# A vision-tower kernel on one core: set-up loads reordered, weight products put into the first step, and the order inside a step changed

## The chip, the cores and the metric

The kernel runs on one core of one Trainium2 chip. Its engines are TensorE (PE: matrix products and transposes; PEld is its load of weights), VectorE (DVE), ScalarE (ACT), GpSimd (POOL) and SyncE (SP, which issues transfers). Each works through its own list of instructions in order and waits for the others by semaphores. The metric is the time of one execution in microseconds of device time.

## The reference

64 images of 2 x 104 x 104 are shifted four ways by 4 pixels and stacked to 10 channels, normalised over the whole stack, multiplied by `gamma`, added to `beta` and convolved in 8 x 8 patches to 169 tokens of 128. Then an attention layer with exponential features and a feed-forward layer in which each token goes to 2 of 8 experts, both behind a layer norm and added to their input:

```
normed = (concat - mean) * rsqrt(var + EPS) * gamma + beta      # statistics over the 10 shifted channels
h = conv(normed, W, stride 8) + b                               # (64, 169, 128)
xn = layernorm(h);  q, k, v = heads(xn @ Wqkv.T)                # 8 heads of 64
qf = exp((q * scale) @ proj.T);  kf = exp(k @ proj.T)
out = (qf @ (kf.T @ v)) / (qf @ sum(kf) + 1e-6)
h = h + out @ Wout.T + bout
y = layernorm(h); top-2 of y @ Wg; softmax of the two           # expert: silu(y @ W[e]) * (y @ V[e]) @ W2[e]
h = h + sum over the two experts of weight * expert(y)
```

## The kernel before, in words

The program has three stages. The **set-up** loads the first group of 8 images, the constants and the weights; computes the image statistics of group 0 (`image_stats`, `image_var`, `image_shift`; GpSimd does the root); turns `gamma`, `beta` and the convolution weights with transposes (`turn_maps`; results `gam`, `bT`, `wct`); folds `proj` into the query and key weights (`qk_mm`, L470, split into a high and a low part `wqp`, `wkp`), and the value weights into the output weights (`vo_mm`, L480, result `wvo`); and makes the patches of group 0 in seven **front pieces**: TensorE transposes normalised rows (L433), VectorE multiplies them by `gam` into `patches` (L761). `cbeta`, the convolution of beta, comes from five products at L492.

The **steps** n = 0 to 34 are a software pipeline over 32 pairs of images. In one step four pairs are in work: pair n (`a`: convolution L555, first layer norm, tokens `xtok`, L878), pair n-1 (`b`: query features in four products `q_feature(0..3)` and key features in three `k_tokens(0..2)`, L643 to L645, each followed by an exponential on ScalarE, then the context), pair n-2 (`c`: the denominators `d8`, L548; VectorE makes their reciprocals `rparts`; `broadcast(0..3)`, L506, spreads them over partitions; `normalise(0..3)`, L812, multiplies; the output products L605; second layer norm) and pair n-3 (`d`: choice of experts, and rows scattered to DRAM by GpSimd). Steps go in groups of four (k = 0 to 3). Beside them runs the front of the next group: statistics in k = 0, and its pieces in k = 1, 2, 3 at the four places `front(0..3)` of a step. The order of every engine is written out by hand in its own `step` function. TensorE uses banks 4 and 5 in turn for the features, banks 7 and 1 for the broadcasts.

The **experts** stage (from about 700 us) is a loop over 92 tiles of sorted rows. It isn't touched.

Transfers of the set-up are issued by SP, by ACT (half of the images) and by POOL (`gamma`, `beta`). The second group of images is issued by SP at its step 0, once `norm_done` has come to 3 (first group normalised). ScalarE sums up that group with `image_sums` (L1014 to L1024) and `image_squares` (L1030, L1032).

## Time and profile before

| | us |
|---|---|
| median of 3 runs (1181.48 to 1183.8) | 1181.81 |
| the profiled execution, its own time | 1181.96 |
| its span, first to last instruction | 1180.2 |
| first convolution (end of set-up) | from 41.35 |
| convolution of step 1, of step 2 | from 57.59, 74.91 |
| PE busy | 1086.5 (92%) |
| DVE, ACT, POOL busy | 877.7, 559.5, 630.3 |

All times are microseconds from the span's start. In a timeline a row is a run of like instructions: start, length, engine, line, operation, out<-in, form, count, and in brackets how long the engine had been idle before it and whose instruction ended that. Matrix products are pipelined, so successive rows of PE overlap: the time that one takes from TensorE is the distance to the next start.

### The profile page before, as it was taken

How to read it: one execution, taken by the hardware profiler on the slowest of the kernel's cores; microseconds unless marked ns; L12 is line 12 of the kernel's file. 1: busy time of each engine (PE TensorE's matmuls, PEld its weight loads, DVE VectorE, ACT ScalarE, POOL GpSimd, SP SyncE). 2: the span in 40 equal slices, each digit the busy share in tenths (PEclk: the TensorE clock that was granted, in tenths of full speed). 3: DMA queues.
4: the chain of work that ended last, by engine and by line, in shares of the span. 5: the costliest groups of instructions: out<-in, count | busy, mean ns of one | idle time of the engine just before them, and what ended most of it. 6: DMA issues, size and time to landing. Idle time of an engine off the chain costs nothing.

```text
span 1180.2 us, 30003 instructions
## 1 busy us (share of the span) xinstructions
PE 1086.5 (92%) x8568; PEld 918.4 (78%) x8569; DVE 877.7 (74%) x3313; ACT 559.5 (47%) x1303; POOL 630.3 (53%) x666
## 2 busy tenths in 40 slices
PE   2699999999999999999999728999999999999994
PEld 2567777777677777777777528999999999999994
DVE  4448788787787878878867666777777777777773
ACT  3243634535436354354333314555555555555551
POOL 2001535354535354545354653777777777677774
PEclk9799999999999999999999958999999999999998
DMA  9252130120301312201010432443444444444442
...
DMA packets 75793, 65.56 MB, mean 56 GB/s; under 512 B 12382, under 2 KB 66718, under 8 KB 75712
## 3 DMA queue, kind: packets, MB, share of 16 engines
...
q14 instruction: 40, 0.33, 0.1%
...
## 4 chain that ended last, share of the span: by engine, by line
PE 68%; issue 13%; DVE 8%; POOL 3%; DMA 1%; ACT 1%; POOLq 0%; DVEq 0%; ACTq 0%; SPq 0%
PE bank L1278 22%; PE bank L1290 13%; PE bank L605 7%; PE bank L669 4%; PE bank L656 3%; PE bank L662 3%; PE bank L555 3%; PE bank L643 2%; DVE patches L761 2%; DVE xtok L878 2%; PE bank L433 2%; DVE attn L812 2%; PE bank L1266 2%; POOL rstd L1150 2%; PE bank L644 2%
## 5 line engine op out<-in xcount | busy, mean ns | idle before, releaser
L1405 POOL DMA_INDIRECT out_rows<-yo,dest x184 | 329.0, 1788 | 139.7 <-issue 94.1
L1278 PE MATMUL bank<-xT_e,wv 128*128 128x256 f32 x2208 | 289.3, 287 | 0.9 <-DVE xT_e L1355 0.9
L1278 PEld LDWEIGHTS bank<-xT_e,wv 128*128 128x128 f32 x2208 | 272.4, 190 | 1.3 <-DVE xT_e L1355 1.3
L1175 POOL DMA_INDIRECT sorted_rows<-xrow_all,sloti x192 | 187.6, 977 | 62.2 <-issue 54.9
L1329 ACT ACTIVATE sil<-bank 128x256 f32<-128x256 f32 x368 | 141.7, 385 | 160.4 <-PE bank L1278 160.4
L1290 PE MATMUL bank<-w,hid 128*128 x1472 | 179.5, 275 | 1.0 <-DVE hid L1362 1.0
L1148 POOL TENSOR_SCALAR vare<-mv 128x3 f32<-128x3 f32 x64 | 12.5, 195 | 303.3 <-issue 249.4
L1290 PEld LDWEIGHTS bank<-w,hid 128*128 128x128 f32 x1472 | 171.6, 192 | 1.2 <-issue 1.2
L1362 DVE TENSOR_TENSOR hid<-sil,bank 128x256 f32<-128x256 f32 x368 | 145.3, 417 | 29.0 <-ACT sil L1329 25.0
L1344 DVE TENSOR_TENSOR wv<-wv_all,wv 128x1024 fp32r<-128x1024 f32 x92 | 112.8, 1226 | 64.6 <-PE bank L1278 62.8
L1313 ACT CAST wv<-wv_all 128x1024 fp32r x92 | 96.2, 1046 | 38.0 <-issue 30.1
L1088 ACT ACTIVATE attn<-bank 128x256 f32<-128x256 f32 x128 | 49.4, 386 | 131.1 <-PE bank L645 131.1
L555 PE MATMUL bank<-patches,wct 128*128 128x338 f32 x320 | 101.9, 466 | 2.3 <-DVE patches L761 2.3
L761 DVE TENSOR_TENSOR patches<-bank,gam 128x416 f32<-128x416 f32 (+3 forms) x160 | 71.7, 503 | 26.4 <-PE bank L433 25.5
L605 PE MATMUL bank<-attn 128*128 128x169 f32 x512 | 83.6, 317 | 7.1 <-DVE attn L812 7.1
L605 PEld LDWEIGHTS bank<-attn 128*128 128x128 f32 x512 | 76.0, 193 | 13.4 <-DVE attn L812 13.2
L555 PEld LDWEIGHTS bank<-patches,wct 128*128 128x128 f32 x320 | 59.7, 194 | 31.5 <-issue 4.3
L1103 ACT ACTIVATE attn<-bank 128x512 f32<-128x512 f32 x96 | 57.3, 598 | 51.5 <-PE bank L645 50.3
L669 PE MATMUL bank<-wvo,attn 128*64 128x136 f32 x1024 | 75.9, 287 | 1.9 <-ACT attn L1123 1.0
L1083 ACT COPY attn<-bank 128x272 f32<-128x272 f32 x128 | 50.0, 390 | 42.6 <-PE bank L669 39.6
L1123 ACT COPY attn<-bank 128x512 f32<-128x512 f32 x32 | 18.7, 586 | 103.9 <-PE bank L662 103.9
L656 PE MATMUL bank<-attn,xtok 128*128 128x512 f32 x128 | 67.9, 612 | 0.0
...
## 6 DMA issues: line engine op xcount, KB each, us to landing
...
```

Of the source, the lines that this page charges most:

```text
L555: t = pe.matmul(bank[1][:, 0:PT], wct[:, q], patches[:, par, q, 2 * k:2 * k + 2].rearrange("p b t -> p (b t)"), start=(q == 0), stop=(q == 4))
L605: t = pe.matmul(bank[7][:, TOK * i:TOK * i + TOK], mm[:, pc, i, j, 0:D], qf[:, pc, j, TOK * i:TOK * i + TOK], start=(j == 0), stop=(j == 3))
L656: pe.matmul(bank[(6, 1)[i]][:, :], xtok[:, p, i], kf[:, i], start=True, stop=False)
L669: t = pe.matmul(o_[64 * (h % 2):64 * (h % 2) + 64, col:col + D + HEADS], gT[:, i, NF * h:NF * h + NF], wvo[:, h], start=True, stop=True)
L1175: po.indirect_dma_start(sorted_rows, bass.IndirectOffsetOnAxis(sloti[:, p, j, ch:ch + 1], 0), xrow[:, p, j, ch], None).then_inc(s(f"scatte ...
L1278: q = pe.matmul(bank[fc][:, TT * m:TT * m + TT], wv[:, w, w_, m, cols], xT[:, p, x_], start=(w_ + x_ == 0), stop=(w_ == 1))
L1290: q = pe.matmul(bank[4 + p][:, D * a:D * a + D], hid[:, p, fc, 128 * a:128 * a + 128], w2[:, bass.ds(e, 1), fc].rearrange("p e n -> p (e n ...
L1313: ac.copy(wv[:, w, 0].rearrange("p m n -> p (m n)"), wv_all[:, bass.ds(e, 1)].rearrange("p e m n -> p (e m n)")).then_inc(s("w_high"), 1)
L1329: ac.activation(sil[:, fc % 2], bank[fc][:, 0:TT], ACT.Silu).then_inc(s("silu_done"), 1)
L1344: ve.tensor_tensor(wv[:, w, 1].rearrange("p m n -> p (m n)"), wv_all[:, bass.ds(e, 1)].rearrange("p e m n -> p (e m n)"), wv[:, w, 0].rear ...
L1362: ve.tensor_tensor(hid[:, p, fc], sil[:, fc % 2], bank[fc][:, TT:2 * TT], ALU.mult).then_inc(s("h_done"), 1)
L1405: po.indirect_dma_start(out, bass.IndirectOffsetOnAxis(dest[:, p, a:a + 1], 0), yo[:, p, a], None, compute_op=ALU.add).then_inc(s(f"added{ ...
```

## The change

On SP the set-up loads come in another order: images, then only the first 358 columns of the constants (the segment `mhalf` is moved up; the rest comes later under a semaphore of its own, `kept_in`), `gamma`, `proj`, the rows, the convolution weights, `beta`, and only then the attention weights. `gamma` and `beta` leave POOL's queue for SP's. VectorE does the image statistics ahead of gamma. TensorE no longer makes the folded weights between the front pieces: `query_key_weights` and `output_weights` run inside step 0, and what VectorE and ScalarE do for them too (`late_weights`, and `image_sums` of group 1 behind `output_weights`). In every step, TensorE's order of query products, broadcasts and key products is another, VectorE's `normalise` calls are spread out, and of `normal_rows` only the small `scaled_gaps` stays early: the rest comes behind `front(2)`.

```diff
-            sp.dma_start(cst[:], const[:, 0:NKEPT]).then_inc(s("const_in"), 16)
-            sp.dma_start(wc_raw, convw.rearrange("e (g c) y x -> e g (c y x)", g=5)).then_inc(s("wc_in"), 16)
+            sp.dma_start(cst[:, 0:NEARLY], const[:, 0:NEARLY]).then_inc(s("const_in"), 16)
+            load_map(sp, graw, gamma, s("gamma_in"))
             for t in range(2):
...
+            load_rows(sp, 0)
+            sp.dma_start(wc_raw, convw.rearrange("e (g c) y x -> e g (c y x)", g=5)).then_inc(s("wc_in"), 16)
+            load_map(sp, braw, beta, s("beta_in"))
+            sp.dma_start(convb_sb[:], convb.rearrange("(d a) -> d a", a=1)).then_inc(s("convb_in"), 16)
+            sp.dma_start(qkv_raw, wqkv.rearrange("(t j e) d -> e t j d", t=3, e=128)).then_inc(s("qkv_in"), 16)
             sp.dma_start(wo_raw, wout.rearrange("o (j e) -> o j e", j=4)).then_inc(s("wo_in"), 16)
-            load_rows(sp, 0)
-            sp.dma_start(qkv_raw, wqkv.rearrange("(t j e) d -> e t j d", t=3, e=128)).then_inc(s("qkv_in"), 16)
-            sp.dma_start(wg_sb[:], wg).then_inc(s("wg_in"), 16)
-            sp.dma_start(convb_sb[:], convb.rearrange("(d a) -> d a", a=1)).then_inc(s("bias_in"), 16)
-            sp.dma_start(bout_sb[:], bout.rearrange("(d a) -> d a", a=1)).then_inc(s("bias_in"), 16)
+            sp.dma_start(cst[:, NEARLY:], const[:, NEARLY:NKEPT]).then_inc(s("kept_in"), 16)
             sp.dma_start(selr, const[:, NKEPT:]).then_inc(s("sel_in"), 16)
             sp.dma_start(tokid[:], const[:, SEG["tok"][0]:SEG["tok"][1]]).then_inc(s("tok_in"), 16)
+            sp.dma_start(wg_sb[:], wg).then_inc(s("wg_in"), 16)
+            sp.dma_start(bout_sb[:], bout.rearrange("(d a) -> d a", a=1)).then_inc(s("bout_in"), 16)
...
-            sp.wait_ge(s("const_in"), 16)
-            sp.dma_start(sorted_rows[E * CAP:E * CAP + TT].rearrange("(a p) n -> p a n", a=2), pad).then_inc(s("pads_out"), 16)
...
+                if n == 1:
+                    sp.wait_ge(s("kept_in"), 16)
...
             pe.wait_ge(s("const_in"), 16)
+            image_stats(0)
+            pe.wait_ge(s("pj_in"), 32)
...
             pe.wait_ge(s("gamma_patched"), 1)
             for half in range(2):
                 turn_maps(bank[5 + half], 0, half).then_inc(s("gamma_mm"), 1)
-            image_stats(0)
...
+            front(0)
             pe.wait_ge(s("wc_in"), 16)
...
-            front(0)
             front(1)
-            pe.wait_ge(s("qkv_in"), 16)
-            pe.wait_ge(s("pj_copied"), 2)
+            front(2)
             pe.wait_ge(s("gam_copied"), 2)
-            for t in range(2):
-                for j in range(4):
...
-            front(2)
             pe.wait_ge(s("beta_patched"), 1)
             turn_maps(bank[6], 1, 0).then_inc(s("beta_mm"), 1)
-            pe.wait_ge(s("wo_copied"), 2)
...
-            for jj in range(2):
...
-            pe.wait_ge(s("wg_in"), 16)
...
             front(4)
-            front(5)
+            pe.wait_ge(s("wc_copied"), 2)
             pe.wait_ge(s("beta_copied"), 2)
             for g in range(5):
...
+            front(5)
             front(6)
-            pe.wait_ge(s("vo_copied"), 2)
...
+            def query_key_weights():
+                pe.wait_ge(s("qkv_in"), 16)
...
+                        mm_ = pe.matmul(bank[4 + t][:, 128 * j:128 * j + 128], qkv_raw[:, t, j], pjT, start=True, stop=True)
+                    mm_.then_inc(s("qk_mm"), 1)
+                pe.wait_ge(s("wo_in"), 16)
...
+                    mm_ = pe.transpose(bank[6][:, 128 * j:128 * j + 128], wo_raw[:, j], ident)
+                mm_.then_inc(s("wo_mm"), 1)
...
+            def output_weights():
+                pe.wait_ge(s("wo_copied"), 2)
...
+                        mm_ = pe.matmul(bank[6 + jj][:, 256 * (j % 2):256 * (j % 2) + 256], wv_c[:, j],
...
+                pe.matmul(bank[2][:, 384:384 + E], ones, wg_sb[:], start=True, stop=True).then_inc(s("gate_mean"), 1)
...
                 if b:
-                    for j in range(2, 4):
-                        pe.wait_ge(s("q_exp"), 4 * mb + j - 1)
-                        q_feature(j)
+                    pe.wait_ge(s("q_exp"), 4 * mb + 1)
+                    q_feature(2)
+                if d and not a and not b:
+                    rank()
+                if c:
+                    pe.wait_ge(s("rden_ready"), mc + 1)
+                    broadcast(0)
                 if a:
...
+                if n == 0:
+                    query_key_weights()
+                if b:
+                    pe.wait_ge(s("q_exp"), 4 * mb + 2)
+                    q_feature(3)
                 front(0)
-                if d and not a and not b:
-                    rank()
                 if c:
-                    pe.wait_ge(s("rden_ready"), mc + 1)
-                    broadcast(0)
-                    if a:
-                        pe.wait_ge(s("h1_ready"), n + 1)
                     broadcast(1)
...
+                for j in range(NCH):
+                    if b:
+                        if j < 2:
+                            pe.wait_ge(s("q_exp"), 4 * mb + 3 + j)
+                        else:
+                            pe.wait_ge(s("k_exp"), NCH * mb + 1)
                         k_tokens(j)
-                for j in range(2, 4):
-                    if c:
-                        pe.wait_ge(s("qn_done"), 4 * mc + j - 1)
-                        broadcast(j)
-                    if b and j < NCH:
-                        pe.wait_ge(s("k_exp"), NCH * mb + j - 1)
-                        k_tokens(j)
+                    if c and j < 2:
+                        pe.wait_ge(s("qn_done"), 4 * mc + j + 1)
+                        broadcast(j + 2)
...
+                if n == 0:
+                    output_weights()
...
+            image_var(0)
+            ve.wait_ge(s("gamma_in"), 16 * 5)
...
+            image_shift(0)
...
-            image_var(0)
-            ve.wait_ge(s("wc_mm"), 1)
-            ve.tensor_copy(wct[:, 0:4].rearrange("p g k -> p (g k)"), bank[1][:, :]).then_inc(s("wc_copied"), 1)
-            image_shift(0)
...
-                    ve.wait_ge(s("qkv_in"), 16)
-                    for j in range(4):
...
-            for t, scale in ((0, QS), (1, 1.0)):
-                ve.wait_ge(s("qk_high"), t + 1)
...
+                    ve.wait_ge(s("wc_mm"), 1)
+                    ve.tensor_copy(wct[:, 0:4].rearrange("p g k -> p (g k)"), bank[1][:, :]).then_inc(s("wc_copied"), 1)
...
+            def output_weights():
+                ve.wait_ge(s("qkv_in"), 16)
+                for j in range(4):
+                    t = ve.tensor_scalar(wv_c[:, j], qkv_raw[:, 2, j], qkv_raw[:, 2, j, D - 1:D], None, ALU.subtract)
...
+                ve.wait_ge(s("wo_mm"), 1)
+                for h in range(2):
+                    ve.tensor_copy(woT[64 * h:64 * h + 64, :, h], bank[6][64 * h:64 * h + 64, :].rearrange("p (j n) -> p j n", j=4)
...
+            def late_weights():
+                for t, scale in ((0, QS), (1, 1.0)):
+                    ve.wait_ge(s("qk_high"), t + 1)
...
+                    ve.scalar_tensor_tensor(out=lo, in0=bank[4 + t][:, :], scalar=scale, in1=hi.bitcast(F32),
...
+                ve.tensor_copy(ident_gate[:, 0:D], ident)
+                ve.wait_ge(s("kept_in"), 16)
...
+                ve.tensor_copy(pick_head[:], selr[0:104].rearrange("p (j f) -> p j f", j=4)).then_inc(s("pick_copied"), 1)
+                ve.wait_ge(s("gate_mean"), 1)
+                ve.scalar_tensor_tensor(out=ident_gate[:, D:], in0=bank[2][:, 384:384 + E], scalar=-1.0 / D, in1=wg_sb[:],
...
+                def scaled_gaps():
+                    ve.wait_ge(s("ln2_rstd"), md + 1)
+                    ve.tensor_tensor(gaps[:], gap[:], rstd[:, 1], ALU.mult).then_inc(s("gap_ready"), 1)
...
-                if d and a:
-                    normal_rows()
...
+                if d and a:
+                    scaled_gaps()
...
+                if c:
+                    normalise(0)
                 if a:
                     ve.wait_ge(s("h1t_done"), n + 1)
                     norm_stats(lambda ch: bank[2][:, D * ch:D * ch + D], 0, n, s("ln1_bn"), s("ln1_mv"))
+                if n == 0:
+                    output_weights()
                 if c:
-                    normalise(0)
                     normalise(1)
                 front(0)
+                if c:
+                    normalise(2)
...
                 if c:
-                    normalise(2)
                     normalise(3)
...
+                if n == 0:
+                    late_weights()
...
+                if d and a:
+                    normal_rows()
...
-                ac.wait_ge(s("qk_mm"), half + 1)
-                ac.mul((wqp, wkp)[half][:, 0], bank[4 + half][:, :], (QS, 1.0)[half]).then_inc(s("qk_high"), 1)
...
+            def query_key_weights():
+                for t in range(2):
+                    ac.wait_ge(s("qk_mm"), t + 1)
+                    ac.mul((wqp, wkp)[t][:, 0], bank[4 + t][:, :], (QS, 1.0)[t]).then_inc(s("qk_high"), 1)
...
+            def output_weights():
+                for jj in range(2):
+                    ac.wait_ge(s("vo_mm"), jj + 1)
+                    ac.copy(wvo[:, 4 * jj:4 * jj + 4, 0:D], bank[6 + jj][:, :].rearrange("p (h n) -> p h n", h=4)
...
-                if fr and k == 0:
+                if n == 0:
+                    query_key_weights()
+                if fr and k == 0 and n > 0:
                     image_sums(g + 1)
...
+                if n == 0:
+                    output_weights()
+                    image_sums(g + 1)
...
-            for raw, src, done in ((graw, gamma, s("gamma_in")), (braw, beta, s("beta_in"))):
-                for q in range(5):
-                    po.dma_start(raw[NP1 * q:NP1 * (q + 1)], src[C * q:C * q + C].rearrange("c (y k) x -> y c k x", k=PATCH)
```

TensorE, step 2, behind the third query product of pair 1 (bank 4); before, the fourth query product, the transposes of `h1T`, both broadcasts and then keys:

```order
L643 MATMUL bank5<-xT,wqp 128x362
L644 MATMUL bank5<-xT,wqp 128x362
L645 MATMUL bank5<-xT,wqp 128x362
L568 MATMUL bank2<-cst,h1T 128x128 x3
L506 MATMUL bank7<-rparts,pick_head 128x340
L506 MATMUL bank1<-rparts,pick_head 128x340
L643 MATMUL bank4<-wkp,xT 128x512
L644 MATMUL bank4<-wkp,xT 128x512
L645 MATMUL bank4<-wkp,xT 128x512
L643 MATMUL bank5<-wkp,xT 128x512
L644 MATMUL bank5<-wkp,xT 128x512
L645 MATMUL bank5<-wkp,xT 128x512
```

and now (the three lines of a product, L643 to L645, are L664 to L666 here, the broadcast is L522):

```order
L522 MATMUL bank7<-rparts,pick_head 128x340
L589 MATMUL bank2<-cst,h1T 128x128 x3
L664 MATMUL bank5<-xT,wqp 128x362
L665 MATMUL bank5<-xT,wqp 128x362
L666 MATMUL bank5<-xT,wqp 128x362
L522 MATMUL bank1<-rparts,pick_head 128x340
L664 MATMUL bank4<-wkp,xT 128x512
L665 MATMUL bank4<-wkp,xT 128x512
L666 MATMUL bank4<-wkp,xT 128x512
L522 MATMUL bank7<-rparts,pick_head 128x340
L664 MATMUL bank5<-wkp,xT 128x512
L665 MATMUL bank5<-wkp,xT 128x512
```

The first broadcast moved ahead of the `h1T` transposes, the fourth query product behind them, and each later broadcast stands behind one key product instead of two.

ScalarE, end of the set-up and step 0, before (`wqp`, `wkp`, `wvo` are the folded weights, `edges`/`edge_out`/`colsum` the statistics of group 1):

```order
L1066 COPY patches<-bank6 128x7x5x13
L1070 ACTIVATE wqp<-bank4 128x512
L1066 COPY patches<-bank6 128x6x5x13
L1070 ACTIVATE wkp<-bank5 128x512
L1073 COPY wvo<-bank3 128x4x128
L1073 COPY wvo<-bank1 128x4x128
L1014 ACTIVATE edges<-raw44 112x16x4 x2
L1021 ACTIVATE nrm44,colsum<-raw44 112x1664
L1024 ACTIVATE edge_out,colsum<-edges 112x128
L1115 CAST xT<-bank3 128x384
L1030 ACTIVATE nrm44,colsum<-raw44 112x1664
L1032 ACTIVATE edge_out,colsum<-edges 112x128
```

and now:

```order
L1105 COPY patches<-bank6 128x6x5x13
L1112 ACTIVATE wqp<-bank4 128x512
L1112 ACTIVATE wkp<-bank5 128x512
L1161 CAST xT<-bank3 128x384
L1117 COPY wvo<-bank6 128x4x128
L1117 COPY wvo<-bank7 128x4x128
L1053 ACTIVATE edges<-raw44 112x16x4 x2
L1060 ACTIVATE nrm44,colsum<-raw44 112x1664
L1063 ACTIVATE edge_out,colsum<-edges 112x128
L1069 ACTIVATE nrm44,colsum<-raw44 112x1664
L1071 ACTIVATE edge_out,colsum<-edges 112x128
```

The folded weights moved to either side of the `xT` copy of step 0, and the sums of group 1 behind them.

VectorE, step 0 from its first convolution, before:

```order
L862 TENSOR_TENSOR h1T<-bank1,cbeta 128x256
L862 TENSOR_TENSOR h1T<-bank1,cbeta 128x2x41
L767 BN_STATS bns<-bank2 128x6 x3
L770 BN_AGGR mv<-bns 128x2 x3
L878 TENSOR_SCALAR xtok<-bank2,mv,rstd 128x128 x3
L890 MEMSET xtok 128x3
L892 TENSOR_TENSOR xT<-bank3,xT 128x384
L703 TENSOR_SCALAR part<-colsum,cst 112x2
L706 SCALAR_TENSOR_TENSOR part<-colsum,cst,part 112x2
```

and now:

```order
L891 TENSOR_TENSOR h1T<-bank1,cbeta 128x256
L891 TENSOR_TENSOR h1T<-bank1,cbeta 128x2x41
L781 BN_STATS bns<-bank2 128x6 x3
L784 BN_AGGR mv<-bns 128x2 x3
L801 TENSOR_SCALAR patches<-xrow_all 128x128 x4
L805 COPY patches<-bank6 64x4x128 x2
L914 TENSOR_SCALAR xtok<-bank2,mv,rstd 128x128 x3
L925 MEMSET xtok 128x3
L927 TENSOR_TENSOR xT<-bank3,xT 128x384
L812 SCALAR_TENSOR_TENSOR wqp<-bank4,wqp 128x512
L812 SCALAR_TENSOR_TENSOR wkp<-bank5,wkp 128x512
```

The value weights (L801) and the turned output weights (L805, which wait for TensorE) now stand ahead of `xtok`, and the low halves of `wqp` and `wkp` behind `xT`.

## Rows read from the trace of the kernel before

**Rows 1.** The page, part 4: the chain that ended last, shares of the span.
```profile
PE 68%; issue 13%; DVE 8%; POOL 3%; DMA 1%; ACT 1%; POOLq 0%; DVEq 0%; ACTq 0%; SPq 0%
```

**Rows 2.** Window of step 5; busy us (instructions) of each engine, TensorE clock, DMA.
```profile
210.50:230.16 19.66, 19.04 (x149) 14.02 (x145) 16.45 (x76) 10.73 (x23) 9.41 (x15) 1.00 0.10 31
```

**Rows 3.** Timeline of step 5: start, length, engine, line, operation.
```profile
210.50 3.11 PE L555 MATMUL bank<-patches,wct 128*128 128x338 f32 x10
...
213.70 0.58 DVE L862 TENSOR_TENSOR h1T<-bank,cbeta 128x256 f32<-128x256 f32 x2
...
213.95 0.33 PE L643 MATMUL bank<-xT,wqp 128*128 128x362 f32 x1
...
214.44 0.49 PE L568 MATMUL bank<-cst,h1T 128*128 128x128 f32 x3
...
214.69 0.56 PE L506 MATMUL bank<-rparts,pick_head 104*128 104x340 f32 x2
...
215.09 0.40 PE L643 MATMUL bank<-wkp,xT 128*128 128x512 f32 x1
...
216.04 1.24 ACT L1103 ACTIVATE attn<-bank 128x512 f32<-128x512 f32 x2 [0.89 <-PE bank L645]
...
218.36 0.92 DVE L812 TENSOR_TENSOR attn<-attn,bank 128x338 f32<-128x338 f32 x2
...
218.52 0.53 PE L649 MATMUL bank<-cst,xtok 128*128 128x128 f32 x3
...
219.33 2.56 PE L605 MATMUL bank<-attn 128*128 128x169 f32 x16 [0.28 <-DVE attn L812]
```

**Rows 4.** Timeline of step 7, TensorE alone.
```profile
258.31 0.49 PE L649 MATMUL bank<-cst,xtok 128*128 128x128 f32 x3
258.64 0.52 PE L433 MATMUL bank<-cst,nrm 104*128 104x104 f32 x4
```

**Rows 5.** Waits in steps 4 to 30: us in total, times, longest.
```profile
PEld bank L605 <- DVE attn L812: 10.4, 20, 0.5
```

**Rows 6.** Timeline of step 32, TensorE alone.
```profile
663.87 0.42 PE L506 MATMUL bank<-rparts,pick_head 104*128 104x340 f32 x1 [0.43 <-DVE attn L812]
```

**Rows 7.** Timeline of the set-up.
```profile
18.25 1.89 DVE L696 TENSOR_REDUCE colsum<-raw 112x1 f32<-112x1664 f32 x1 [2.58 <-DMA raw<-in_x]
...
24.25 3.72 ACT L1042 ACTIVATE nrm<-raw,imgshift,imgrstd 112x832 f32<-112x832 f32 x3 [3.59 <-DVE imgshift L719]
...
25.16 1.41 DVE L744 COPY patches<-bank 64x512 f32<-64x512 f32 x2
...
28.77 3.50 PE L470 MATMUL bank<-patches,xrow_all 128*128 128x128 f32 x16
...
32.92 1.94 PE L480 MATMUL bank<-patches 128*128 128x256 f32 x8
...
39.51 1.57 ACT L1021 ACTIVATE nrm<-raw 112x1664 f32<-112x1664 f32 x1
...
41.35 4.77 PE L555 MATMUL bank<-patches,wct 128*128 128x338 f32 x10 [2.27 <-DVE patches L761]
```

**Rows 8.** Windows of the set-up, columns as in rows 2.
```profile
0.00:10.00 10.00, 0.00 (x0) 0.01 (x1) 4.42 (x13) 1.30 (x2) 6.90 (x16) 1.00 0.72 127
10.00:18.00 8.00, 0.00 (x0) 0.00 (x1) 1.02 (x1) 0.00 (x0) 0.00 (x0) 1.00 1.05 161
```

**Rows 9.** Timeline of step 0 and the start of step 1.
```profile
46.85 0.55 PE L568 MATMUL bank<-cst,h1T 128*128 128x128 f32 x3 [0.74 <-DVE h1T L862]
...
49.91 1.05 DVE L878 TENSOR_SCALAR xtok<-bank,mv,rstd 128x128 f32<-128x128 f32 x3 [1.36 <-POOL rstd L1150]
...
52.33 1.59 ACT L1030 ACTIVATE nrm<-raw 112x1664 f32<-112x1664 f32 x1
...
54.87 0.54 PE L419 MATMUL bank<-part,cst 112*112 112x2 f32 x2 [2.96 <-DVE part L706]
```

**Rows 10.** Window in step 0, columns as in rows 2.
```profile
51.00:56.00 5.00, 2.03 (x8) 1.63 (x9) 1.23 (x5) 2.35 (x5) 0.00 (x0) 0.50 0.00 0
```

104 lines of the change are left out of this document (47 added, 57 removed).

## The prediction

> **What bounds the kernel now.** The chain that ended last comes first: TensorE holds 68% of it, issue 13%, VectorE 8% [rows 1], so a gain has to shorten TensorE's list or a stretch in which TensorE waits. The window of one step shows which: in step 5 TensorE is busy for 19.04 of 19.66 us at the full clock of 2.4 GHz, VectorE for 16.45 [rows 2]. The experts' loop isn't touched. Two places are left: small waits inside a step, of which there are some thirty, and the 57 us up to the convolution of step 1. The reader is to look in the timelines for the distance between starts on TensorE, which shows a stall even where the idle time in brackets is small.
>
> **Inside a step.** The second layer norm's `xtok` stands between VectorE's second and third `normalise`, so the last one ends late: two of them run 218.36 to 219.28, and the output products begin at 219.33, although the three transposes before them began at 218.52 [rows 3]. In step 7, where a front piece stands between, the same three take 0.33 [rows 4]. So TensorE stalls 219.33 - 218.52 - 0.33 = 0.48; I take 0.45, since the switch of kind costs a little too. The list of waits has this one 20 times, 10.4 us in all on the weight loads [rows 5]: every step with k = 0, 1, 2. With steps 2, 31 and 28 to 30 outside or inside that window, 23 steps have it.
>
> The new order does `normalise(2)` while VectorE would wait for GpSimd's root, so only `normalise(3)` (half of 0.92) stands behind `xtok`. Laid out for step 5 from rows 3: third query product until 213.95 (there the fourth began), first broadcast until 214.15 (two took 215.09 - 214.69 = 0.40). `h1T` is written 213.70 to 214.28, so the transposes now wait until about 214.33, a new stall of 0.2 that the fourth query product covered before. Then transposes 0.25 to 0.33, fourth query product 0.5, broadcast, and from there the same work as before. The fourth product moved behind costs 214.44 - 213.95 = 0.5, the broadcast moved ahead gives back 0.2, the transposes begin 0.1 earlier, a further change between kinds of product costs 0.1: TensorE reaches the output products's place 0.3 later in pure work, or 0.25 without the small stall in front of the third broadcast that goes. The stall of 0.45 goes fully, as `normalise(3)` then ends near 218.8 and TensorE comes at 218.95. And two products no longer queue up for one `normalise`, another 0.1. Net gain 0.45 + 0.1 - 0.25 = 0.3 (bounds 0.1 and 0.45) in 23 steps: **-7.0**.
>
> In k = 3 with a front piece (7 steps) there is no stall to win [rows 4] and the price stays: 0.25 each, **+1.8** (0 to 3).
>
> `normal_rows` (0.85, three products on VectorE) leaves the head of the step, where it stood ahead of `dsum`, for the place behind `front(2)`. VectorE has 3.2 us free in the step [rows 2], and the row work now lies where it waits for ScalarE's copy of h2; its end is late by at most 0.85, and the same 0.85 no longer stands ahead of the reciprocals. GpSimd copies the rows later and comes to its root of the second norm up to 0.7 later; `scaled_gaps`, which waits for that root, has moved behind the `h1T` addition, over 3 us on. I cost it at 0; if the cover were gone it would be 0.7 in each of the steps, the upper end of a bad case below. The wait for the scatters in `place` is met a step earlier.
>
> In step 32 there is no convolution to hide things: the second key product now stands behind the third broadcast, which waits for VectorE until 663.87 [rows 6]; that product takes 0.7 (0.49 for the 362 columns of a query product [rows 3], here 512). **+0.7**. Steps together: -7.0 + 1.8 + 0.7 = **-4.5**.
>
> **The set-up.** Statistics need the images and a piece of the constants. They landed by 18.25 [rows 7]. By 18 us 10 x 127 + 8 x 161 KB = 2.56 MB had moved [rows 8]. Now eight images (80 KB each), the edges (53 KB) and 358 columns of constants (183 KB) stand at the heads of two queues: 0.86 MB, which at 161 GB/s from 2 us on are in at 7.3. Transfers don't fill all engines alike, and I take 10 (bounds 7.5 and 13): images 8.25 earlier.
>
> On this the skill has two sentences. The Trainium skill, DMA: Bandwidth & Descriptors, "Issuing engines are not separate DMA queues", says that transfers of all issuing engines interleave on the same 16; the trace's share of 1.05 with three queues open agrees, so two queues lose nothing. The section on why a DMA increments its semaphore by 16 says that a copy from SP or ACT runs on the largest number of engines up to 16 that divides its outer size: 12 for an image, 13 for a map. No run here shows that; as an estimate by that page the images would come at 2 + 0.86 / (0.161 x 12/16) = 9.1 instead of 7.3, inside my bounds, and the maps, moved to SP, would gain nothing from the move.
>
> From landing to the first normalisation are 24.25 - 18.25 = 6.0, unchanged: 16.0. From there to the first convolution were 17.1 [rows 7]. The query/key products (3.50) and value/output products (1.94) leave this stretch, which would make it 11.7. But `beta` now lies behind 0.86 MB, `gamma` (0.43), `proj` (0.03), the rows (0.68) and the convolution weights (0.33), with its own 0.43 some 2.8 MB deep, which is 19 us at the same rate and by the uneven filling more likely 23; its copy, maps, the five products of `cbeta` and two front pieces with VectorE's multiplications behind them follow. That makes about 34.5, and bounds of 28 and 37. Conv starts **-6.9**.
>
> Step 0 gives it back. Before, from the start of the `h1T` transposes to that of the statistics of group 1, which stand ahead of step 1 on TensorE, were 54.87 - 46.85 = 8.0 [rows 9]. Two additions:
> 1. `xtok` waits for 0.55 of transposes, the query/key products, four transposes and VectorE's 1.41 [rows 7]. At full clock (1.75 + 0.5) it starts 4.2 after 46.85, at half (3.50 + 1.1) 6.6; before 3.06. So +1.15 or +3.5.
> 2. Between `xtok` and ScalarE's squares were 52.33 - 49.91 = 2.4. Now: `xtok` 1.05, transposes 0.5, output products 1.94 (or twice), copy 0.54, sums of group 1 about 2.3 (1.57 of it in rows 7, where ScalarE did them in idle time): 6.3 or 8.7. So +3.9 or +6.3.
>
> Together +5.1 at 2.4 GHz, +9.8 at 1.2. Low-halves and other late weights on VectorE lie beside the sums. The convolution itself, 4.77 here [rows 7] against 3.11 in step 5 [rows 3], may gain 1.3 at full clock. Sum for the set-up: -6.9 - 1.3 + 5.1 = -3.1, or -6.9 + 9.8 = +2.9. The clock decides: in step 0 it is granted at 0.50 with TensorE busy for 2.03 of 5.00 us [rows 10]. TensorE: Matmul & The Clock Gate (the Trainium skill, "What's actually happening") says that the clock is set by how busy the array has recently been; the row agrees, and by that rule the products at the front of step 0 run warm behind the convolution and the output products, behind an idle wait, cold. That is in between, and I take **-1** (bounds -5 and +5).
>
> **Sum.** -4.5 - 1 = -5.5 on the profiled execution's 1181.96 (span 1180.2 and 1.8 around it), which is 0.15 above the median: **1176.4**.
>
> **The rivals.**
> - *The set-up pays.* If images land at 8 and the clock stays up, it gives -6 rather than -1, and the steps 0.35 each: 1170. For it: SP's order of need. Against: the serial stretch of step 0, over 5 us at either clock.
> - *The steps give nothing*: `h1T` is the wait that takes the place, 0.45 in all of 30 steps instead of 0.2, and with it the late k products. Then steps +1, set-up -1: 1182. For it: VectorE wrote `h1T` right behind the reciprocals, so any delay goes through. Against: the list of steps' waits has it small.
> - *Slower: ScalarE's exponentials.* The second key product needs the exponential of the fourth query product, now begun 1 us later, and the third key product that of the first key, in two banks. From rows 3: query product ends 215.4, its exponential (0.5, by its columns and the 0.62 of a key's) 215.95, while TensorE comes at 216.2; margin 0.25. The two key exponentials took 1.24, so the next margin is 0.2. If the exponentials come 0.5 later than I lay out, both margins are gone and each step loses 0.6 instead of gaining 0.3: 30 x 0.3 + 7 x 0.6 more, with the set-up +2: 1191. It decides from 0.3 us on.
>
> **Chances.** My forecast 50%, set-up pays 22%, no gain 16%, exponentials 12%. A difference below 0.2% (2.4 us) can't be told from none here. The forecast (1172 to 1180) lies nearly all below 1179.4; with the first rival that makes faster 0.70, same 0.17, slower 0.13. The range takes in the bounds of the set-up and half of the slower case: 1168 to 1184.
>
> **What would show it.** Output products start 0.33 behind the `xtok` transposes in k = 0 to 2, with a gap of 0.2 before the `h1T` transposes; group distance 0.7 us shorter over four steps. Image landing near 10, first convolution near 34.5, step 1's statistics product near 54. It is wrong if the gap between third query product and transposes is over 0.4, if TensorE waits for ScalarE before a key product, or if step 1's convolution starts over 3 us from 57.

## The result and the profile after

The changed kernel took 1170.55 us (median of 4 runs, 1169.45 to 1171.41), the kernel before 1182.12 beside it (1181.48 to 1183.8): ratio 0.9897, 95% interval 0.9882 to 0.9913, 11.6 us less where 5.5 had been forecast. The profiled execution took 1170.11 us, with a span of 1168.3. In the chain that ended last TensorE went from 68% to 84% [rows 1]. This share is no measure of the gain: it moved by 16 points and the span by 1%.

```profile
PE 84%; DVE 6%; issue 3%; DMA 2%; ACT 2%; SPq 1%; POOL 1%; POOLq 0%; ACTq 0%; DVEq 0%
```

The gain inside a step shows in step 5, to be read against [rows 3]. Those rows and [rows 2] are headed step 5, but the convolution that they begin with, at 210.50, is that of step 9 ([rows 4] is step 11, not 7). The comparison holds all the same: step 5 of the kernel before, from 132.75 on, also took 19.66, and reached the transposes of `xtok` after 8.03. First the window after (distance, then busy us of TensorE, its weight loads, VectorE, ScalarE, GpSimd; clock, DMA share, GB/s), 19.29 where 19.66 was [rows 2]:

```profile
130.12:149.41 19.29, 18.93 (x149) 14.01 (x145) 15.99 (x74) 10.76 (x23) 9.63 (x16) 1.00 0.10 32
```

Then its timeline on TensorE (start, length, line, operation). L522 is the broadcast, L589 the transposes of `h1T`, L670 those of `xtok`, L626 the output products:

```profile
133.56 0.31 PE L522 MATMUL bank<-rparts,pick_head 104*128 104x340 f32 x1
133.90 0.55 PE L589 MATMUL bank<-cst,h1T 128*128 128x128 f32 x3
134.20 0.42 PE L664 MATMUL bank<-xT,wqp 128*128 128x362 f32 x1
...
138.23 0.49 PE L670 MATMUL bank<-cst,xtok 128*128 128x128 f32 x3
138.58 1.70 PE L626 MATMUL bank<-attn 128*128 128x169 f32 x10
```

The output products start 0.35 behind the transposes of `xtok`, not 0.81. The transposes of `h1T` begin 0.34 behind the first broadcast, which takes 0.16 (134.78 to 134.94 for the next): the new wait is 0.18, and 0.2 was forecast. Up to the transposes of `xtok` TensorE needs 8.11 from the start of the step and needed 8.02 [rows 3]: the new order costs it 0.09, not 0.25. The waits of the whole span say the same (us in total, times, longest), first before, then after:

```profile
PEld bank L605 <- DVE attn L812: 13.2, 25, 1.0
PEld bank L506 <- DVE attn L812: 9.9, 25, 1.2
...
PEld bank L568 <- DVE h1T L862: 3.5, 11, 1.4
```

```profile
PEld bank L589 <- DVE h1T L891: 11.0, 32, 1.3
...
PEld bank L522 <- DVE attn L840: 2.5, 2, 1.6
...
PEld bank L626 <- DVE attn L840: 1.0, 1, 1.0
```

Two waits for `normalise` nearly go, that of the output products (13.2 to 1.0) and that of the third broadcast (9.9 to 2.5); the one for `h1T` (3.5 to 11.0) takes their place, shorter and in every step.

The set-up after, to be read against [rows 7] and [rows 9]:

```profile
11.12 1.89 DVE L714 TENSOR_REDUCE colsum<-raw 112x1 f32<-112x1664 f32 x1 [5.44 <-DMA raw<-in_x]
...
22.81 1.58 ACT L1101 COPY wv_all<-attn 65x1664 f32<-65x1664 f32 x1 [1.32 <-DMA attn<-in_L_tok_beta]
...
33.68 4.76 PE L572 MATMUL bank<-patches,wct 128*128 128x338 f32 x10 [2.29 <-DVE patches L775]
...
44.92 1.89 PE L506 MATMUL bank<-patches 128*128 128x256 f32 x8
...
47.64 1.58 ACT L1060 ACTIVATE nrm<-raw 112x1664 f32<-112x1664 f32 x1
...
49.69 1.59 ACT L1069 ACTIVATE nrm<-raw 112x1664 f32<-112x1664 f32 x1
...
52.31 0.54 PE L430 MATMUL bank<-part,cst 112*112 112x2 f32 x2 [5.37 <-DVE part L724]
...
55.03 4.25 PE L572 MATMUL bank<-patches,wct 128*128 128x338 f32 x10
```

The images are there at 11.12 (was 18.25), the first convolution starts at 33.68 (41.35), step 1's at 55.03 (57.59). Step 0 gives back 5.1 of 7.7, and the row for L430 shows where most of it goes: TensorE idles for 5.37 behind the output weights while ScalarE sums and squares group 1.

Three marks divide every run here: the convolution of step 2, the last convolution (step 31's), the end of the span.

```
start of conv, us      step 2    step 31   between     behind
before                 74.91     637.74    562.83      542.5
after                  73.09     626.08    552.99      542.2
```

So 1.8 of the 11.9 in the span lie ahead of step 2, 9.8 in steps 2 to 30, 0.2 behind. These are marks of one profiled execution each. How far they move by themselves, kernels with the same code in a stretch show: between the marks 562.8 and 563.2 with the old steps (before, and s2 below), 552.8 to 553.4 with the new ones (changed kernel, s1 and i2 below). A single step can be 0.3 off.

### The profile page after: what moved, and what is told of

Its sections match the earlier page's. It is cut to its first block, busy times and chain, and to the rows that moved or that the text cites. A ratio compares the mean times of both kernels' runs of the same rounds, so it can differ in the third digit from the quotient of the medians.

```text
span 1168.3 us, 29989 instructions
## 1 busy us (share of the span) xinstructions
PE 1082.7 (93%) x8568; PEld 920.1 (79%) x8569; DVE 879.2 (75%) x3313; ACT 560.7 (48%) x1303; POOL 624.7 (53%) x656
## 4 chain that ended last, share of the span: by engine, by line
PE 84%; DVE 6%; issue 3%; DMA 2%; ACT 2%; SPq 1%; POOL 1%; POOLq 0%; ACTq 0%; DVEq 0%
PE bank L1324 22%; PE bank L1336 13%; PE bank L572 8%; PE bank L626 5%; PE bank L690 4%; PE bank L664 4%; PE bank L677 4%; PE bank L666 4%; PE bank L665 4%; DVE patches L775 3%; PE bank L683 2%; PE bank L444 2%; PE bank L565 2%; PE bank L522 2%; PE bank L1312 2%
## 5 line engine op out<-in xcount | busy, mean ns | idle before, releaser
L626 PE MATMUL bank<-attn 128*128 128x169 f32 x512 | 81.2, 311 | 0.6 <-DVE attn L840 0.6
L690 PE MATMUL bank<-wvo,attn 128*64 128x136 f32 x1024 | 75.9, 287 | 2.3 <-ACT attn L1172 1.4
L626 PEld LDWEIGHTS bank<-attn 128*128 128x128 f32 x512 | 75.5, 192 | 2.0 <-DVE attn L840 1.0
L1147 ACT ACTIVATE attn<-bank 128x512 f32<-128x512 f32 x96 | 57.3, 598 | 33.8 <-PE bank L666 33.8
L690 PEld LDWEIGHTS bank<-wvo,attn 128*64 128x64 f32 x1024 | 56.7, 136 | 14.6 <-ACT attn L1127 6.9
```

The source lines that it names most:

```text
L626: t = pe.matmul(bank[7][:, TOK * i:TOK * i + TOK], mm[:, pc, i, j, 0:D], qf[:, pc, j, TOK * i:TOK * i + TOK], start=(j == 0), stop=(j == 3))
L690: t = pe.matmul(o_[64 * (h % 2):64 * (h % 2) + 64, col:col + D + HEADS], gT[:, i, NF * h:NF * h + NF], wvo[:, h], start=True, stop=True)
```

## Experiments

Ratios are to the kernel before on the same chip, with 95% intervals. On two chips every kernel was slower, that before too (1254 and 1281 us), and the traces of the changed ones there show VectorE and ScalarE starting late from step 4 on. Ten of the eighteen runs fell there, and of them only times up to the end of step 3 are used. s1 is all step edits on the old set-up, s2 the new set-up alone, s3 and s5 one step edit each, i2 the changed kernel with one more move:

```
kernel (runs)     step 2   step 3   ratios on these two chips
s1 (1)            19.02    19.36    0.9979
s2 (2)            19.51    19.32    0.9987, 0.9930
s3 (3)            19.11    19.30    0.9963, 0.9975, 0.9979
s5 (2)            19.50    19.54    1.0212, 1.0276
i2 (2)            step 2 begun at 71.86, 70.56; ratios 0.9799, 0.9815
before, elsewhere 19.52    19.30
```

These early steps already tell s3 (0.4 gained in step 2) from s5 (nothing there, 0.24 lost in step 3). What had been expected, in the order of the runs, is quoted here; whatever it says of the end of the kernel these runs leave open.

The first four were to settle where the gain lies. Beyond step 3 they settle nothing: the "9 us faster" of s1 and s3 did not show on that chip, and s5's loss did:

> The kernel before with all the changes to the order inside a step (TensorE's, the early third normalisation, the late row work) and its old set-up. Theory T: the steps' gain stands by itself and is 9.8 us from step 2 on, so this run is 9 to 10.5 us faster than the kernel before (about 1172), with the output products 0.33 behind the transposes of xtok in k = 0 to 2. Rival A (my forecast's sizes hold and the rest of the gain comes from the set-up, whose early arrivals help the steps too): 4 to 5.5 us faster (about 1177). Rival B (most comes from the two parts together): under 3 us.

> The changed kernel with the steps in the order of before: the set-up's change alone. Theory T: step 1's convolution starts 2.6 us earlier and its own step is 0.7 longer at the low clock, so 1.5 to 2.5 us faster than the kernel before (about 1180). Rival A: 6 us or more faster (about 1175). Rival B: between -1 and +1 us, its gain given back within the first steps.

> The kernel before with one thing moved: VectorE does the third normalisation ahead of xtok instead of behind it. TensorE's order stays. Theory T (the stall of 0.48 behind the transposes of xtok and a slow restart of 0.1 are what the steps gained, and the new order on TensorE costs and gives nothing): 23 steps x 0.4 to 0.55 = 9 to 12 us faster. Rival P (TensorE's new order is needed, since in the old one the third normalisation is asked of VectorE while it has the reciprocals' and xtok's inputs to serve, and xtok comes later for it): xtok is 0.45 late and its transposes wait as long, so within 2 us of the kernel before.

> The kernel before with TensorE's new order alone; VectorE's and the set-up stay. Theory T (price of the order per step is 0.0 to 0.1, as read in the changed kernel; the stall of 0.48 stays, for VectorE's third normalisation still stands behind xtok): between 1 us faster and 3 us slower. Rival Q (the order itself gives: two broadcasts no longer queue up): 3 to 6 us faster. Rival R (my forecast's price of 0.25 in 30 steps holds and was hidden by VectorE's change): 6 to 8 us slower.

Run again, with the same late starts, with steps 2 and 3 within 0.02 of the first time (s2, s3 and s5). i2 was ahead of the kernel before even so, by 2.0 and 1.9%:

> The kernel before with one thing moved: VectorE does the third normalisation ahead of xtok. Run again, since its first run was disturbed from step 4 on; in step 2, not disturbed, it took 19.10 (all step changes 19.02, before 19.52) and in step 3 19.29 (19.39, 19.30). Theory T (this one move carries the steps' gain, TensorE's new order adds 0.1 to 0.2 in some steps and costs 0.08 in k = 3): 23 x 0.4 = 9 us less up to the last convolution, that is 1173.5, give or take 3 us for the clock in the last steps. Rival P (TensorE's order is needed in k = 0 and 1): under 5 us.

> The kernel before with TensorE's new order alone. In step 2, not disturbed, it took 19.50 (before 19.52), in step 3 19.53 (19.30). Theory T: no gain in k = 0 to 2, a loss of 0.2 in k = 3, so 7 x 0.2 = 1.4 us later at the last convolution, 1183 to 1185. Rival R (my forecast's price of 0.25 in all 30 steps): 1189 or more. Rival Q (the order itself gives): under 1180.

> The changed kernel with the steps in the order of before. Disturbed the first time; its step 2 began at 75.10 there, against 74.91 in the kernel before and 73.09 in the changed one, because step 0 took 23.07 instead of 21.35 with its first microseconds at the low clock. Theory T (the set-up's gain is 1.8 at step 2 in the changed kernel, of which the clock's phase in step 0 can take all): 1180 to 1182. Rival A (the set-up holds what is missing, 5 us): 1177 or less.

> The changed kernel with two moves in step 0: ScalarE makes the image sums of group 1 while it waits for the transposes of xtok, instead of behind the copies of the output weights, and TensorE takes their statistics product in step 1 behind the first two query products, instead of at the end of step 0. If the serial stretch behind the output weights (copy, sums, squares, product) is what step 0 gives back, step 1's query products begin 4 to 5.5 us earlier than 53.08 and the kernel takes 1165 to 1167. Rival: the low weights on VectorE or the low clock hold step 1 anyway, 1169 to 1171.

> The kernel before with one thing moved: VectorE does the third normalisation ahead of xtok. On a chip without the late starts from step 4 on. All step changes together measured 9.3 us less at the last convolution and 6.5 at the end. Theory T (this one move carries the steps' gain): 23 x 0.35 to 0.4 = 8 to 9 us less at the last convolution, so 1173 to 1177 at the end, as the clock falls in the last steps. Rival P (TensorE's order is needed in k = 0 and 1): under 5 us less at the last convolution.

> The changed kernel with ScalarE's image sums of group 1 ahead of the copy of xT in step 0, and TensorE's statistics product in step 1 behind two query products. In its first run step 2 began at 71.86 (changed kernel 73.09), though its first convolution was 1.3 later. Undisturbed: 1.2 to 2.5 us less than the changed kernel, 1168 to 1169.5. Rival: the clock in the last steps takes it back, 1170 to 1173.

The marks of the eight runs on other chips, without late starts, of one profiled execution each:

```
kernel                        us     step 2  step 31  between  change  behind
s1 all step edits           1176.0    75.12   628.47   553.35   -9.5   545.3
s3 early normalise(2)       1172.5    76.48   630.54   554.06   -8.8   540.7
s5 TensorE's order          1187.9    74.10   641.57   567.47   +4.6   543.9
s6 s1 with rows in place    1176.3    75.41   630.94   555.53   -7.3   542.3
s4 late rows                1182.0    75.20   636.47   561.27   -1.6   544.5
s2 set-up alone             1182.5    75.49   638.66   563.17   +0.3   543.2
i2 changed, sums early      1167.0    70.28   623.10   552.82  -10.0   541.8
b1 i2, TensorE as before    1182.5    68.18   637.05   568.87   +6.0   541.7
```

**All step edits on the old set-up (s1).** It is the change's diff for the two step functions of TensorE and VectorE, and no other line.

> The kernel before with all the changes to the order inside a step and its old set-up, run again. In the first round of this kernel the kernel before itself took 1254 us instead of 1182, since from step 4 on vector and scalar engines started 0.7 to 1.1 us after what they waited for had ended, and TensorE fell to the low clock in several steps; in steps 2 and 3, not disturbed, it was 0.5 shorter in k = 2 and even in k = 3. Undisturbed, theory T (the steps' gain stands by itself): 9 to 10.5 us faster, about 1172. Rival A (my forecast's sizes): 4 to 5.5 us faster. If the disturbance is there again, ratio 0.996 to 1.000 as before.

Measured: 1176.02 against 1182.53, ratio 0.9943 (0.9926 to 0.9959), 6.5 us. Between the marks all 9.5 us are there, so the steps' gain needs no new set-up. The end keeps 6.5, because behind the last convolution it takes 2.9 more. The window of the first 41 us there shows a clock of 0.88, then those of the kernel before (0.94), of the changed kernel (0.92) and of i2 (0.93):

```profile
628.47:669.47 41.00, 35.90 (x256) 25.77 (x252) 25.88 (x129) 13.11 (x35) 22.75 (x32) 0.88 0.31 90
```

```profile
637.74:678.74 41.00, 34.38 (x258) 24.30 (x254) 27.91 (x139) 13.05 (x35) 22.71 (x32) 0.94 0.32 93
...
626.08:667.08 41.00, 35.17 (x258) 25.42 (x254) 26.78 (x134) 13.08 (x35) 22.65 (x32) 0.92 0.31 93
...
623.10:664.10 41.00, 34.08 (x258) 24.62 (x254) 28.36 (x141) 13.08 (x35) 22.73 (x32) 0.93 0.33 93
```

s1, the changed kernel and i2 have the same instructions from the last convolution on and take 545.3, 542.2 and 541.8 behind it. The new order is therefore not what makes s1's 2.9. A low clock in step 32 is part of it: the output products of that step start 31.3, 29.6 and 27.9 behind the last convolution.

Both theories' bounds were missed at the end; at the last convolution theory T's sum was right.

**The set-up alone (s2).** The changed kernel with the steps' two functions in their old order.

> The changed kernel with the steps in the order of before: the set-up's change alone, on a chip without late starts. Step 2 began at 75.10 and 74.44 in the first two runs (before 74.91, changed kernel 73.09). Theory T (the set-up is worth 0 to 2 us, by the clock in step 0): step 2 at 74.4 to 75.1, 1180 to 1182.5. Rival A (the set-up holds a gain of 5 us that shows only at the end): 1177 or less. The sum of this run's gain and that of all step edits (6.5) should be 7 to 9; the rest of the changed kernel's 11.6 would then be the clock in the last steps.

Measured: 1182.47 against 1183.41, ratio 0.9992 (0.9982 to 1.0003): no difference that can be told. Its first convolution starts at 34.99, and step 2 at 75.49, 2.4 later than in the changed kernel, on nearly the same instructions in step 0. The rows of TensorE there:

```profile
34.99 4.80 PE L572 MATMUL bank<-patches,wct 128*128 128x338 f32 x10 [2.18 <-DVE patches L775]
...
46.28 3.46 PE L506 MATMUL bank<-patches 128*128 128x256 f32 x8
...
55.23 0.53 PE L430 MATMUL bank<-part,cst 112*112 112x2 f32 x2 [5.26 <-DVE part L724]
```

The output weights' eight products took 3.46 here, and 1.89 in the changed kernel. The window of 45 to 50 us has a clock of 0.66 here and 1.00 there. Those 1.6 and the first convolution's 1.3 make 2.9, of which step 1 (17.54 for 18.06) gives back 0.5. The old set-up has such a spread too: over all chips, kernels with it began step 2 between 74.10 and 77.39 in twelve profiled executions (mean 75.4), kernels with the new one between 73.09 and 75.49 in four (mean 74.5). So the set-up is worth about 1 us, 0 to 2 by the clock that step 0 is granted, and the 1.8 of the two marks is at the favourable end. Rival A falls.

The parts do not add up to the whole: by their medians s2's 0.9 and s1's 6.5 make 7.4 of the changed kernel's 11.6. By the marks of the profiled executions the two parts make 4.7 of 11.9, and of the 7.2 that are missing 3.9 lie behind the last convolution, 2.6 ahead of step 2 and 0.7 between. The steps are nearly additive, the two stretches with changing clocks are not. That the clock alone makes their difference isn't shown.

**The third normalisation alone (s3).**

```diff
                 front(0)
+                if c:
+                    normalise(2)
                 if a:
                     ve.wait_ge(s("ln1_rstd"), n + 1)
...
                 if c:
-                    normalise(2)
                     normalise(3)
```

> The kernel before with the early third normalisation alone, on a chip without late starts. Step 2 took 19.11 and step 3 19.30 in all three runs so far (before 19.52 and 19.30). Theory T: 0.4 in the 23 steps with k = 0 to 2, 9 us less at the last convolution, 1173 to 1176 in all. Rival P (in k = 0 and 1 TensorE's order is needed): under 5 us less there, 1178 or more.

Measured: 1172.47 against 1182.2, ratio 0.9915 (0.9898 to 0.9931), 9.7 us for one call moved, 0.5 more than theory T's bounds. Steps 4, 5, 6 took 18.62, 19.27, 19.31 (before 19.02, 19.66, 19.74), step 7 19.31, as before. The wait of the output products has gone (1.3 for 13.2), the two others stay nearly as before:

```profile
PEld bank L506 <- DVE attn L812: 10.8, 25, 2.0
...
PEld bank L568 <- DVE h1T L862: 3.6, 11, 1.4
...
PEld bank L605 <- DVE attn L812: 1.3, 2, 1.0
```

About 0.40 in every step with k = 0 to 2, theory T. Rival P falls: `xtok` waits for GpSimd's root anyway (0.51 in step 9 of the kernel before), and the normalisation lies in that wait. This one move has 8.8 of the 9.5 us of all step edits between the marks. That it beats them at the end is no merit of its steps: 540.7 behind the last convolution, 1.8 less than before, of which its own stall in step 31 is 0.4.

**TensorE's order alone (s5).** TensorE's hunk of the change, everything else as before.

> The kernel before with TensorE's new order alone, on a chip without late starts. Step 2 took 19.50 and step 3 19.54 in both runs so far (before 19.52 and 19.30). Theory T (no gain in k = 2, price 0.2 in k = 3, little in k = 0 and 1): 7 x 0.2 = 1.4 us more at the last convolution, 1183 to 1185 in all. Rival R (price 0.25 in all 30 steps): 1189 or more. Rival Q (the order itself gives in k = 0 and 1): under 1180.

Measured: 1187.91 against 1182.2, ratio 1.005 (1.0033 to 1.0067), 5.7 us more, between theory T's 1185 and rival R's 1189, and 4.6 and not 1.4 at the last convolution. In k = 3 it costs 0.2 to 0.3 (19.52 to 19.62), as T had it; k = 0 costs about 0.4 (19.39 to 19.44, once 19.57), which neither had; k = 1 and 2 next to nothing. Step 5 shows how:

```profile
137.38 0.40 PE L643 MATMUL bank<-wkp,xT 128*128 128x512 f32 x1
137.62 0.39 PE L644 MATMUL bank<-wkp,xT 128*128 128x512 f32 x1
137.85 0.40 PE L645 MATMUL bank<-wkp,xT 128*128 128x512 f32 x1
138.48 0.42 PE L506 MATMUL bank<-rparts,pick_head 104*128 104x340 f32 x1 [0.23 <-DVE attn L812]
...
141.15 0.49 PE L649 MATMUL bank<-cst,xtok 128*128 128x128 f32 x3
141.47 0.74 PE L605 MATMUL bank<-attn 128*128 128x169 f32 x4
```

A key product takes 0.23 here, so the third broadcast could start at 138.08 and starts at 138.48: a stall of 0.40. The output products now follow in 0.32. The stall was not removed, it moved, from the output products to the third broadcast. In step 4 the same stall of 0.40 is there, and the transposes of `h1T` start 0.56 behind the first broadcast, 0.19 more than in step 5. Of the 0.4 that k = 0 costs half lies ahead of the output products, and what makes the other half isn't shown. The waits for that broadcast rise from 9.9 to 21.5 us:

```profile
PEld bank L506 <- DVE attn L812: 21.5, 32, 2.6
PEld bank L572 <- DVE h1T L862: 12.7, 32, 1.3
```

**The row work (s6, s4).** s6 is s1 with `normal_rows` (and with it `scaled_gaps`) at the head of the step again; s4 is the kernel before with these alone moved, `normal_rows` behind `front(2)`.

> The kernel before with TensorE's new order and the early third normalisation, but the row work (normal_rows) left at the head of the step on VectorE. Measured so far in step 3 (k = 3, with rows): kernel before 19.30, TensorE's order alone 19.54, everything 19.39, third normalisation alone 19.30. Theory V (the row work, moved away from the head, lets VectorE reach the reciprocals and the h1T addition 0.85 earlier, which covers TensorE's new wait for h1T): step 3 at 19.5 to 19.55 here, step 2, which has no rows yet, at 19.02 as with everything, and 30 steps x 0.1 to 0.2 = 3 to 6 us later at the last convolution than with everything. Rival W (the rows are off the path, as I had costed them; it is the normalisation that covers): step 3 at 19.39 and no difference.

> The kernel before with the row work alone moved behind front(2). Theory V: in the old order the fourth query product covers the wait for h1T, so the move gives little by itself: step 3 at 19.25 to 19.30, steps 28 to 30, which have less to cover with, 0.1 to 0.4 shorter; 0 to 3 us faster in all. Rival X (the end of the late row work holds GpSimd's root up): steps 0.3 longer, 8 us slower.

Measured: s6 1176.34 against 1182.21, ratio 0.9964 (0.9951 to 0.9977); s4 1182.03, ratio 1.0001 (0.9991 to 1.001). In s6 steps 3, 5 and 6 took 19.38, 19.28 and 19.23, as in s1 (19.39, 19.29, 19.24): rival W is right there. But step 4 took 18.83 (s1 18.67) and steps 28 and 29 took 18.82 and 18.53 (18.30 and 18.27). So the move is worth 0.2 in k = 0 and up to 0.5 where no front piece stands between, 2.2 us between the marks, less than theory V's 3 and more than rival W's none. The wait that it shortens is the one for `h1T`. First s1's rows in step 4, then those of s6, where VectorE does the rows ahead of the reciprocals and `h1T`:

```profile
116.98 0.32 PE L506 MATMUL bank<-rparts,pick_head 104*128 104x340 f32 x1
117.31 0.55 PE L572 MATMUL bank<-cst,h1T 128*128 128x128 f32 x3
```

```profile
117.25 0.35 PE L506 MATMUL bank<-rparts,pick_head 104*128 104x340 f32 x1
117.79 0.55 PE L572 MATMUL bank<-cst,h1T 128*128 128x128 f32 x3 [0.18 <-DVE h1T L862]
```

The transposes start 0.33 behind the broadcast in s1 and 0.54 in s6, 0.33 and 0.54 again in step 28. Alone in the old order it gives 1.6 there, and nothing that can be told at the end, inside theory V's 0 to 3; rival X falls.

**Sums and statistics of group 1 (i2).** To test what step 0 gives back, the sums move ahead of the copy of `xT`:

```diff
-                if fr and k == 0 and n > 0:
+                if fr and k == 0:
                     image_sums(g + 1)
...
                 if n == 0:
                     output_weights()
-                    image_sums(g + 1)
```

On TensorE `image_stats(1)` moves from the end of step 0 to behind the first two query products of step 1.

> The changed kernel with ScalarE's image sums of group 1 ahead of the copy of xT in step 0, and TensorE's statistics product behind two query products of step 1. Step 2 began at 71.86 in its first run (changed kernel 73.09). On a chip without late starts: 1.2 to 2.5 us less than the changed kernel's 1170.5, so 1168 to 1169.5. Rival: the clock in the last steps takes it back, 1170 to 1173.

Measured: 1166.99 against 1183.41, ratio 0.9864 (0.9848 to 0.9881), beside 0.9897 of the changed kernel, which ran on another chip: 3.6 us less by its own time. That is less than the 1168 to 1169.5 expected here, and inside the 1165 to 1167 of its first expectation. It is the fastest kernel here. The first query product of step 1 starts at 47.31, 5.8 earlier than in the changed kernel, and the convolution of step 1 at 50.14, 4.9 earlier:

```profile
42.11 1.58 ACT L1062 ACTIVATE nrm<-raw 112x1664 f32<-112x1664 f32 x1
...
44.69 1.89 PE L506 MATMUL bank<-patches 128*128 128x256 f32 x8
...
47.31 0.40 PE L666 MATMUL bank<-xT,wqp 128*128 128x362 f32 x1 [0.60 <-DVE wkp L814]
...
49.73 0.36 PE L430 MATMUL bank<-part,cst 112*112 112x2 f32 x2 [1.19 <-DVE part L726]
```

At step 2 2.8 of the 4.9 are left: from its convolution on step 1 takes 20.14 instead of 18.06. 0.5 of these 2.1 are in the convolution and what follows it directly (clock 0.61 for 0.67). 1.5 are in the last part, from the products with `wvo` (L692, L690 in the changed kernel) to the next query products, which took 4.22 at a clock of 0.60, where the changed kernel took 2.69 at 1.00:

```profile
64.14:68.36 4.22, 4.22 (x37) 3.43 (x37) 1.07 (x3) 1.55 (x4) 0.00 (x0) 0.60 0.76 140
```

```profile
68.49:71.18 2.69, 2.69 (x37) 2.13 (x37) 1.07 (x3) 1.56 (x4) 0.00 (x0) 1.00 0.69 140
```

In both kernels the stretch stands behind the same wait of 1.43 for ScalarE and has the same 37 products; what differs is the clock.

**i2 with TensorE's old step order (b1).** VectorE's new order stays whole.

> The same, with TensorE's order inside a step as in the kernel before, and VectorE's new order (third normalisation early, row work late). With the third normalisation alone the kernel before became 9.7 us faster, with TensorE's new order and the late rows too only 6.5. If TensorE's new order is worth nothing and costs 1 to 3 us in the steps behind the last convolution, where a key product waits for a broadcast: 1165 to 1168, 1 to 3 us less than the run before. Rival (with the late rows TensorE's order is worth 0.7 us at the last convolution): 0 to 2 us slower than the run before.

Measured: 1182.47 against 1183.41, ratio 0.9999 (0.9986 to 1.0013). Both expectations missed, by 13 us and more. Against the changed kernel it gains 5 us up to step 2 and loses 16 between the marks. VectorE's row in step 5:

```profile
131.48 0.51 DVE L842 TENSOR_TENSOR attn<-attn,bank 128x338 f32<-128x338 f32 x1 [0.44 <-PE bank L522]
```

VectorE's new order has a second part, which s3 left out: `normalise(0)` stands ahead of the first norm's statistics. With TensorE's new order its broadcast is ready by then (in the changed kernel it starts at 134.23 with no wait). With the old one the broadcast stands behind the transposes and VectorE waits 0.44. The statistics start 5.05 behind the convolution (4.52 in the changed kernel) and `xtok` 7.47 (6.94), and over the whole span the waits are:

```profile
PEld bank L672 <- DVE xtok L916: 40.6, 32, 2.8
DVE attn L842 <- PE bank L522: 26.2, 32, 1.2
```

The changed kernel has 16.3 in the first of these rows, the kernel before 21.6. So s3's lesson does not extend to the whole of VectorE's order. That it is `normalise(0)` is read from the rows: no run has it alone, and b1 has the late rows as well. s3's single move on i2's set-up has not been run either.

## Why the prediction was right or wrong

**The mechanism in a step was right, the size of its net gain was not.** The step that failed is "Net gain 0.45 + 0.1 - 0.25 = 0.3": its price of 0.25 for TensorE's order measured 0.07 to 0.09, and the net gain 0.43 in the steps 2 to 26 with k = 0 to 2. With it failed the row work, "I cost it at 0". Steps 2 to 30 were forecast at 22 x -0.3 + 7 x 0.25 = -4.9 and gave -9.8. Of the 5.0 between, 2.5 are the 19 steps with 0.43 for 0.3, 1.4 the steps 28 to 30, 1.1 the steps with k = 3. Term by term:
- The stall of 0.45: s3 removes it alone and gains 0.40 a step; the reading from [rows 3] and [rows 5] held. The 0.1 for two products that no longer queue was not measured by itself.
- The price of 0.25, meant for TensorE's order whatever VectorE does: in k = 3 s5 measured 0.2. With VectorE's order changed too it was 0.07 (19.38 for 19.31), and step 5 needed 0.09 more up to the transposes. I had added the delay of single instructions to the sum. The rows of step 5 show the same products with other waits between them: the new one for `h1T`, 0.18, less about 0.1 in front of the third broadcast, which I had taken as 0.05.
- That the order by itself does not remove the stall, but moves it to the third broadcast, I had not seen: s5, +4.6 us. In s6, which adds the early `normalise(0)` and `normalise(2)` to it, this turns into -7.3; which of the two does how much isn't shown. TensorE's hunk can't be costed alone.
- The row work, "I cost it at 0": at the head of a step it stands ahead of `h1T`, for which TensorE now waits. It is worth 0.2 in k = 0 and up to 0.5 in steps 28 to 30, 2.2 us in all (s6). Those three took 18.28 each, where 19.23, 18.92 and 19.01 were, in all 2.3 less and not 0.9.
- k = 3 was forecast at +1.8 for seven steps and gave 0.7.

Over one group (steps 8 to 11) the distance fell from 77.78 to 76.58, by 1.2 and not 0.7.

**Step 32.** +0.7 was forecast for a second key product behind the third broadcast. s5 has the cleanest measure: the third broadcast stands 26.1 behind the last convolution, as before, and the product for the ranks (L524) 28.43 for 27.25, so 1.2, with the added product at the low clock. In the changed kernel the output products of step 32 start 1.3 later behind the last convolution than before (655.70 - 626.08 against 666.07 - 637.74), yet the end behind it is 0.2 shorter. Of the 1.5, 0.7 are the output products of step 33, which took 4.13 and not 4.87, 0.3 a shorter wait in step 34 (4.25 for 4.54), and 0.5 the experts' part (467.2 us for 467.6). None of them is the product that the forecast priced.

**The set-up.** -1 was forecast within -5 and +5; 1.8 were gained at step 2, and the set-up alone shows nothing that can be told. Images: 11.1 for 10, inside the bounds. `beta`: there at 22.8 for 23. First convolution 33.68 for 34.5. Step 0 gave back 5.1, the figure for the high clock, by the mechanism named: `xtok` starts 4.25 behind the transposes of `h1T` (4.2 forecast), and ScalarE's squares 6.25 behind `xtok` (6.3). i2 shows it by taking it away. The 1.3 that a first convolution at full clock was to give did not come: 4.76 for 4.77. Step 1 then took 18.06 for 17.32, which the forecast had left out. On the images, the row of the first 10 us has 127 GB/s at a DMA share of 0.61 (before 0.72 [rows 8]):

```profile
0.00:10.00 10.00, 0.00 (x0) 0.01 (x1) 4.41 (x13) 1.30 (x2) 1.00 (x6) 1.00 0.61 127
```

By 10 us 1.27 MB had moved, more than the 0.86 MB of the images and the first constants, and still the images were not all there: transfers that stand behind them in the queues had taken a part, and the engines had room left. 7.3 was too early for both reasons. The Trainium skill, DMA: Bandwidth & Descriptors, in its section on why a DMA increments its semaphore by 16, lets a copy of an image use 12 engines; by that I had 9.1. The measurement, 11.1, lies behind both 7.3 and 9.1, and no run here takes the rule apart from other causes.

**The clock.** I had weighed its two levels in step 0 and put my forecast between. The profiled executions show it as an alternative: the same eight products took 3.46 in s2 and 1.89 in the changed kernel. The Trainium skill, TensorE: Matmul & The Clock Gate ("What's actually happening"), says that the clock follows how busy the array has recently been; the traces agree as far as low clocks come only in and behind the waits of the set-up and the last steps (1.00 from 200 to 600 us in the kernel before), but in s2 a first convolution 1.3 later went with other products being hit.

**The rivals.** "The set-up pays" gave the right time, 1170, for the wrong reason: it put -6 in the set-up, where there were -1.8, and 0.35 in a step, where there were 0.43. "The steps give nothing" fell: the wait for `h1T` took 0.18 and not 0.45. "ScalarE's exponentials" fell too: TensorE's waits for a key exponential (PEld L664 <- ACT attn L1147) are 0.6 us in the whole span, 2.2 before. The sum of this rival, 1191, was wrong on its own terms: steps that lose 0.6 thirty times, with +2 in the set-up, make about 1202.
